# A graph network on one core: the turned edge features kept as 96 rows, their fourth quarter copied on VectorE

## What is computed

```
# layer 0, a gated convolution
z = concatenate([h[src], h[dst], edge_feats], axis=1)
gate = sigmoid(_bn(z @ W_int + b_int, ...)); upd = softplus(_bn(z @ W_upd + b_upd, ...))
agg = segment_sum(gate * upd, dst)
...
# layer 3, the "classifier" of the change's title
x = concatenate([h[src], edge_attr], axis=-1)
msg = maximum(x @ W1 + b1, 0.0) @ W2 + b2
agg = segment_sum(msg, dst) / count
y = layernorm(h + agg) * gamma + beta
```

## Time and profile before

| | |
|---|---|
| median of three executions | 12515.34 us |
| span of the profiled execution | 12513.0 us (the page gives no other time for it) |
| busy: TensorE matmuls, weight loads | 7973.5 us (64%), 7348.9 us (59%) |
| busy: VectorE, ScalarE, GpSimd | 8105.8 us (65%), 6908.4 us (55%), 5177.6 us (41%) |
| DMA | 3241.49 MB, mean 259 GB/s |
| conv spread: first and last store of `e_turned` | 2462.5 and 3427.0 us |
| classifier's spread: first load of `e_turned`, last matmul with it | 11596.9 and 12012.1 us |

### The profile page before, as it was taken

One profiled execution on the slowest core, in us unless ns is written; L12 is line 12 of the kernel. 1 busy time (PEld: TensorE's weight loads), 2 busy tenths in 40 slices (PEclk: granted clock), 3 DMA queues, 4 the chain that ended last, 5 costly groups with the idle time before them and its releaser, 6 DMA issues. The chain is left out here.

```text
span 12513.0 us, 440619 instructions
## 1 busy us (share of the span) xinstructions
PE 7973.5 (64%) x149673; PEld 7348.9 (59%) x149684; DVE 8105.8 (65%) x17787; ACT 6908.4 (55%) x17614; POOL 5177.6 (41%) x4482
## 2 busy tenths in 40 slices
PE   6444444488856659985766656666666666665765
PEld 6333333388744448885756656565665566565765
DVE  6777777688799989981851753816709437358047
ACT  1222222298855559977117458965469664587530
POOL 2777777544300001110721852706707237345044
PEclk8555555599999989988869779797697786887997
DMA  5555543299977769978939999979989799997997
GB/s 204 168 166 171 166 143 82 81 348 347 338 197 211 210 192 323 322 239 306 343 114 352 290 265 353 291 275 296 278 327 313 223 332 289 291 335 226 369 362 225
DMA packets 1430365, 3241.49 MB, mean 259 GB/s; under 512 B 392074, under 2 KB 973252, under 8 KB 1419042
## 3 DMA queue, kind: packets, MB, share of 16 engines
q1 hardware_dynamic: 1054798, 2289.98, 52.3%
q0 software_dynamic: 331264, 823.09, 25.0%
q10 hardware_dynamic: 44116, 125.96, 3.4%
HBM read 2042.53 MB, written 1129.76 MB: 254 GB/s over the span
## 5 line engine op out<-in xcount | busy, mean ns | idle before, releaser
L1974 POOL DMA_INDIRECT mask_cols<-cols_all,mask_index x864 | 1368.4, 1584 | 1333.3 <-ACT mask_index L1983 1148.2
L521 POOL DMA_INDIRECT rows_s<-place_rec,place_index x1568 | 1637.6, 1044 | 538.4 <-issue 534.1
L596 PE MATMUL place_slot_ps<-place_runs,place_oh_turned 50*128 50x100 f32 x3136 | 726.0, 423 | 1238.3 <-DVE place_runs L635 1220.1
L2122 POOL DMA_INDIRECT hop_x<-cols_all,hop_index x864 | 981.4, 1136 | 1245.0 <-ACT hop_index L2129 924.1
L596 PEld LDWEIGHTS place_slot_ps<-place_runs,place_oh_turned 50*128 50x128 f32 x3136 | 683.1, 327 | 1272.5 <-issue 1272.3
L2138 ACT ACTIVATE hop_parts<-hop_x,mask 128x64 f32<-128x64 f32 x5184 | 1266.1, 336 | 61.1 <-DMA hop_x<-cols_all,hop_index 30.0
L2065 DVE SCALAR_TENSOR_TENSOR mask_hidden<-mask_cols,att 128x448 f32<-128x448 f32 x864 | 538.0, 623 | 1087.1 <-DMA mask_cols<-cols_all,mask_index 1032.0
L2185 PE MATMUL hop_sums_ps<-hop_parts,hop_onehot 128*128 128x64 bf16 x18144 | 882.3, 216 | 478.6 <-DVE hop_parts L2167 397.5
L2185 PEld LDWEIGHTS hop_sums_ps<-hop_parts,hop_onehot 128*128 128x128 bf16 x18144 | 781.8, 113 | 581.5 <-issue 580.2
L1496 POOL DMA_DIRECT2D cm_onehot<-hot_d x288 | 152.1, 528 | 1978.0 <-POOLq L104 1179.4
L2032 PE MATMUL mask_part_ps<-mask_now,mask_turned 128*128 128x64 bf16 x18144 | 907.2, 231 | 33.2 <-issue 20.0
(11 more groups left out here) (397 smaller groups left out, 26043.0 us busy)
## 6 DMA issues: line engine op xcount, KB each, us to landing
cols_all<-att_in_rows SPq DMA_DIRECT2D x216, 896.0 KB
mask_onehot<-hot_s SPq DMA_DIRECT2D x216, 896.0 KB
cols_all<-hop_in_rows SPq DMA_DIRECT2D x216, 896.0 KB
hop_onehot<-hot_s SPq DMA_DIRECT2D x864, 224.0 KB
rows_all<-blank SPq DMA_DIRECT2D x72, 1808.0 KB
ct_u<-rows_all SPq DMA_DIRECT2D x288, 452.0 KB
cm_v<-rows_all SPq DMA_DIRECT2D x288, 448.0 KB
cm_onehot<-hot_d POOLq DMA_DIRECT2D x288, 448.0 KB
```

Of the source, the lines that this page charges most:

```text
L521: nc.gpsimd.indirect_dma_start(m.rows_s.rearrange("p n w -> (p n) w"), bass.IndirectOffsetOnAxis(index[:, j, t:t + 1], 0), rec[:, j, t, :] ...
L596: last = nc.tensor.matmul(slot_ps[b][:, t, 0:2 * NBK], oh_turned[:, b, t, :], runs[:, b, t, :], start=True, stop=True)
L1974: nc.gpsimd.indirect_dma_start(cols[:, n, :], None, table, bass.IndirectOffsetOnAxis(index[:, n, :], 0), compute_op=ALU.add).then_inc(arri ...
L2122: nc.gpsimd.indirect_dma_start(x[:, n, :, :].rearrange("p c f -> p (c f)"), None, table, bass.IndirectOffsetOnAxis(index[:, n:n + 1], 0)). ...
```

## The change

`e_turned` in HBM has 96 rows instead of 128. Conv spread makes the same 128 partitions as before, uses them, and stores the first 96. The classifier's spread loads 96 rows into partitions 0 to 95, and VectorE copies partitions 0 to 31 to 96 to 127, once per batch, before TensorE uses the batch; a semaphore `doubled` tells TensorE.

```diff
@@ stage_conv_spread, SyncE
-                    sp.dma_start(m.e_turned[:, bass.ds(it, 1), :], as_words(e_turned[:, i, :, :])).then_inc(turned_stored[i], 16)
+                    sp.dma_start(m.e_turned[:, bass.ds(it, 1), :], as_words(e_turned[0:3 * EF, i, :, :])).then_inc(turned_stored[i], 16)
@@ stage_mlp_spread
-        spread, taken, gate = (sem(n) for n in ("spread", "taken", "gate"))
+        spread, taken, doubled, gate = (sem(n) for n in ("spread", "taken", "doubled", "gate"))
         with nc.Block() as block:
+            @block.vector
+            def _(dve):
+                def step(it, s, i, k, more, _):
+                    if i == 0:
+                        dve.wait_ge(e_came[s], k * 16 + 16)
+                        if not isinstance(it, int) or it > 11:
+                            dve.wait_ge(spread, it - 8)
+                        dve.sem_inc(gate, 1)
+                    nc.vector.tensor_copy(e_turned[3 * EF:P, s, i, :, :], e_turned[0:EF, s, i, :, :]).then_inc(doubled, 1)
+                each12(dve, step, first=12)
+
...
-                    sp.dma_start(quad_words(e_turned[:, s, :, :, :]), m.e_turned[:, bass.ds(quad * 4, 4), :]).then_inc(e_came[s], 16)
+                    sp.dma_start(quad_words(e_turned[0:3 * EF, s, :, :, :]), m.e_turned[:, bass.ds(quad * 4, 4), :]).then_inc(e_came[s], 16)
...
                     if i == 0:
                         pe.wait_ge(e_came[s], k * 16 + 16)
+                    pe.wait_ge(doubled, it + 1)
                     pe.wait_ge(taken, it + 1)
@@ build
-        m.e_turned = dram("e_turned", [P, NBT, C * P // 2])
+        m.e_turned = dram("e_turned", [3 * EF, NBT, C * P // 2])
```

## The result

The changed kernel took 12596.43 us (median of four runs, 12581.26 to 12608.49), and the kernel before 12511.93 us (four runs too): a ratio of 1.0066, interval 1.0052 to 1.0081, so 65 to 101 us slower. The forecast said 12435, at most 12506. Both touched stages became longer: from first to last store of `e_turned` conv spread took 1027.0 us (964.6 before), from first load to last matmul the classifier's spread took 451.7 us (415.2 before). That is 99 us, and the spans of the two profiled executions differ by 94 (12606.9 and 12513.0), so the rest of the program didn't grow.

What follows compares the result with a forecast made beforehand. The prediction took the DMA queue to bound both spreads. It summed 38 us (load) + 43 us (store) - 1 us (first copy) = 80 us off the 12513.0 us span, plus 2.3 us for the median: 12435 us, range 12412 to 12506.

Steps and rivals of the forecast that it cites:

- What bounds the stages: Both spreads: DMA queue work sets the pace, not latency; DMA share 0.99 in conv spread, 1.01 in the classifier's.
- waits for the landing: Conv spread, L1213 and L1176: most waits, also those named `cs_e_ps`, are for `cs_rec` to land; up to 65.8 us.
- What stands behind the queue: Conv spread: with the queue's lateness gone, ScalarE is the next bound, at 3.12 us per batch.
- What a removed row is worth: Both spreads' transfers: 284 ns for a row of 7168 B, 83.5 ns for one of 1792 B.
- The fit of 16.5 ns + 0.0374 ns per byte: Price of a data packet on SyncE's queue, a line through both spreads' mean packets (239.9 ns and 67.8 ns).
- The sum's two terms: Time saved: 38 us by the classifier's spread's narrower load, 43 us by conv spread's narrower store.
- The copies: Classifier's spread: VectorE's 288 copies take 0.66 us each (0.22 to 1.08), covered by queued DMA work except about 1 us once.
- an exposed copy: Rival, chance 0.06: each quad's first copy delays TensorE, 78 us, total 12513; sign: share below 1.0, TensorE's waits name the copy.
- The ports rival: Chance 0.26: rows 0 to 63 share half the memory paths, so 96 rows save little in both spreads; 12475 (12467 to 12505).
- The narrow rows rival: Chance 0.08: in both spreads narrower transfers cost more per row, losing from 1.33 times the old row time.
- Its example of 1.5 times: Narrow rows at 1.5 times the row time: +20 us in the classifier's spread, +24 in conv spread, total 12559.

Runs made afterwards that it cites:

- rows_32_95: The kernel before with only partitions 32 to 95 of `e_turned` stored and loaded, the others zeroed once; ratio 0.9929, conv spread 926.1 us, classifier's spread 356.9 us.
- short_rows: The kernel before with all 128 rows of `e_turned` stored and loaded, but three quarters of each; ratio 0.9957.
- copy_only: The changed kernel with its transfers left at 128 rows, so only VectorE's copy and TensorE's wait are new; ratio 1.0003 to the kernel before.
- rows_0_63: The kernel before with only partitions 0 to 63 of `e_turned` stored and loaded, the others zeroed once; ratio 0.9996 to the kernel before.
- Load_halves: Store of 128 rows, each quad's load in two transfers (partitions 0 to 63, 64 to 127), with the copy; ratio 1.0068 to the kernel before, classifier's spread 507.3 us.

## Why the prediction was wrong

- *What bounds the stages*: right. Both follow the DMA queue: with the queue's work cut evenly (rows_32_95) conv spread became 38 us shorter and the classifier's spread 58. That most of the waits under the name `cs_e_ps` were waits for the landing was right as well: with the landings earlier they went from 65.8 to 0.8 us at L1213, with the landings later 114.7 of 132.6 us bore the landing's name. What stands behind the queue was put a little low: 890 us for 277 batches of rows_32_95 are 3.21 us each, not 3.12.
- *What a removed row is worth*: this step failed. The fit of 16.5 ns + 0.0374 ns per byte came from stages whose large transfers all have 128 rows, and was used for one of 96. After the change the classifier's packets took 281 ns where the fit gives 236; conv spread's took 69.1 for 66.8, and its DMA engines stood idle for 77 of 1000 us beside 12 of 940. The bytes by themselves gained 54 us, not 81 (short_rows); the narrow shape cost some 140 us on top of that, to end 84 us slower.
- *The sum's two terms* had the wrong sign: -43 was +62 in conv spread, and -38 was +36 in the classifier's spread.
- *The copies*: 0.38 us each, between the bounds and under the 0.66 taken; covered, as said (copy_only). The sign named for an exposed copy, TensorE's waits under its name, came all the same and misled.
- *The ports rival*, at 0.26, had the rule that rows_0_63 and rows_32_95 bear out, but took eight rows on the busiest path as the worst that could be, so it could only gain. Load_halves, with eight there too and 94 us more, shows that this isn't the worst.
- *The narrow rows rival* had the right sign, at 0.08. Its reason ("neighbouring rows then fall to engines that collide") fits the runs but isn't shown, and narrow transfers as such are not dear: rows 32 to 95 paid 240 ns. Its example of 1.5 times gave +44; it was +84. It priced only the narrow rows, while GpSimd's packets cost 7% more too and DMA engines stood idle in conv spread.
- The prediction itself said that no large transfer in the trace had fewer than 128 rows. That was an unknown about the change's main term, and not a detail for a rival.

## What to carry to other kernels

A transfer's price per row, taken from transfers over all 128 partitions, needn't hold for another set of partitions. Here, in two stages that the DMA queue bounds, shorter rows and partitions 32 to 95 paid, and dropping the last quarter cost. Count what one more transfer costs the queue that issues it. When the waits name a new instruction, ask what that instruction waited for.

## What the hardware showed beyond that

A load of 112 rows was slower than one of 128 (480.7 us for the stage on the slower chip, 413 for copy_only on another; by the ratios 1.0037 and 1.0003), and the same 128 rows in two halves slower still (507.3 us). A store of 96 rows on SyncE's queue also slowed GpSimd's transfers by 7%; whether SyncE's own transfers of 128 rows slowed isn't shown, since the rows give only a mean over all of a queue's packets. The DMA share stayed at 1.00 to 1.02 in the classifier's spread in all the stretches shown, from 329 to 406 GB/s: a full share doesn't tell that the engines are moving what they could.
